# Second attention on one core: scores of a key tile added onto those of two tiles back

## The chip, the cores and the metric

One core of a Trainium2 chip runs the whole kernel in one launch. The metric is the device time of that launch in microseconds. The median of three runs is 1237.6 us (1237.28 to 1238.63).

## The reference

Two layers, each an attention times a gate, added to the tokens. 2048 tokens (2 sequences of 1024) of 128 features. Layer one is an attention over the 16 heads of a token and a mixture of experts; layer two, where the change is, is

```python
xn = _layernorm(x, axis=-1)
s = _L1_attn_ref(xn, gamma, w_qkv, w_out)      # RMS norm, then per head
#   q, k, v = rms_norm(xn) @ w_qkv ; q = q * 64 ** -0.5
#   sim = einsum('bhid,bhjd->bhij', q, k) ; attn = softmax(sim) ; out = attn @ v ; out @ w_out
g = _silu(_L1_ffn_ref(xn, ...))                # gated linear units, two hidden layers of 512
x = x + s * g
```

with 16 heads of 64 and 1024 keys for each of 1024 queries of a sequence.

## The kernel before

**Stages.** First norm, router and head attention (to about 220 us), experts (to about 350), second attention (first exponential at 369.8, last at 1084.7), last network. Products that need more than the fast format keeps are made of three: an operand is cut into a high part (F32R, a copy on ScalarE) and a low part (the rest, a subtract), and high x high, low x high and high x low are added in PSUM.

**A step** of the second attention, `m`, is one sequence and one pair of heads: 2 x 8 = 16 steps. It has 16 *slots*: `half` (512 queries) and key tile `j` (128 keys), `slot = 8 * half + j`; and 8 *batches* `b` of two slots. TensorE keeps two score banks, `st_ps[:, slot % 2]`, so that a slot's bank was last that of the slot two back. The engines' orders are written out by hand, batch by batch:

- TensorE (`tensor`): the first maxima product (`tensor_maxima`, L1273: scores of 128 queries against 512 keys into the single buffer `mx_ps`, for a later half or step), the scores of two slots (`tensor_scores`, L1286 to L1292, four products for each of the two heads: high key x high query, high x low, low x high, and minus the row maximum through `minus` and `q_max`), the second maxima product, one unit (`BEFORE`: projections q, k, k, the transposed maxima `tr`, q, v, output, `tr`), the output products of the two slots before (L1306), and in some batches a unit of `AFTER` (denominator, output, v). A maxima product waits on `s_mxr` for VectorE's reduce of the one before. The two matmuls of a line, one for each head, use different rows of the array; the text calls them a pair.
- ScalarE (`scalar`): two exponentials of 1024 columns (`prob`, L1413), then the copies out of the projection bank `pj_ps` (L1371 for `q_hi` and `k_hi`, L1376, L1383) and of `o_ps` (`o_sum`, L1389).
- VectorE (`vector`): reduce of the first maxima (L1463), reciprocals (L1481), `q_max` (L1445), reduce of the second maxima, low parts (`vector_low`, L1439), sums into `y` (L1456), and in batches 1 and 5 the normalizing multiply `o_n` (L1488), whose inputs `o_sum` and `rden` both lie in SBUF.
- GpSimd (`gpsimd`): adds the exponentials of a half into `acc` (L1550, 1024 columns, seven for each half): one in batches 0 and 4, two in each of the others.

Units of step `m + 1` (queries, keys, values) are made in step `m`. The projection bank is handed on by `bank_free`: after a `qk` unit TensorE waits for `vector_low`.

In `experts`, L903 (`x<-x,new`) and L1432 (`w_lo`, the low part of the second attention's weights) are VectorE operations with two SBUF inputs, beside GpSimd's L1052 and L1055.

Of the kernel before, what the change touches and what calls it, by code (L numbers as in the profile page):

```python
# [1067 lines left out]
def second_attention(nc, c, head, e, a, xr, xr_hi, xr_lo, early, pairs, late, at):  # L1068
# [11 lines left out]
    minus = early.sb("minus", [P, P], F32R)  # L1080
# [4 lines left out]
    q_hi, q_lo, k_hi, k_lo = ([place.sb(n, [P, LEN], F32R) for place in (pairs, late)]  # L1085
                              for n in ("q_hi", "q_lo", "k_hi", "k_lo"))
# [89 lines left out]
    def bank_free(pe, turn):  # L1176
# [5 lines left out]
        if u[0] == "qk":  # L1182
            pe.wait_ge(s_lo, 4 * q + QK.index(u) + 1)
# [207 lines left out]
    def scalar_begin(act):  # L1391
# [116 lines left out]
    def vector(dve, m, b):  # L1508
# [13 lines left out]
        if at_b and at_b[1][0] == "qk":  # L1522
# [285 lines left out]
def two_layers(nc, a, out):  # L1808

    with ExitStack() as ctx:  # L1810
# [43 lines left out]
        t2 = second_attention(nc, c, head, e, a, xr, xr_hi, xr_lo, early, pairs, late, at)  # L1854
# [258 lines left out]
```

## Time and profile before

| | |
|---|---|
| median of three runs | 1237.6 us |
| the profiled execution | 1235.84 us |
| its span | 1234.0 us |
| TensorE busy | 1177.2 us (95%) |
| VectorE busy | 850.5 us (69%) |
| GpSimd busy | 755.4 us (61%) |
| ScalarE busy | 576.3 us (47%) |
| mean granted clock of TensorE | 0.985 |

The engines run at once, each through its own list in order, and meet at semaphores. A share of busy time over the whole span mixes the stages; what bounds a stage is read from a stretch of it, and what a wait costs from the instruction that is released last. In the rows PE is TensorE (PEld its weight loads), DVE VectorE, ACT ScalarE, POOL GpSimd; L is a line of the kernel before.

### The profile page before, as it was taken

What the parts mean: (1) busy time and instruction counts of PE and PEld (TensorE: products, weight loads), DVE (VectorE), ACT (ScalarE), POOL (GpSimd) and SP (SyncE); (2) the same over time, 40 slices, a digit from 0 to 9 for tenths busy, and PEclk for the clock granted to TensorE, in tenths of its full rate; (3) what the DMA queues carried; (4) which work ended last, traced back from release to release, by engine and by line L of the source; (5) the groups of instructions that cost most, each with busy time, mean ns of one, the idle gap of its engine ahead of it and who ended that gap; (6) DMA issues with size and microseconds to landing.
All of it is one profiled execution on the core that took longest, in us unless ns stands there. A gap on an engine that the chain in (4) does not pass through costs nothing.

```text
span 1234.0 us, 22455 instructions
## 1 busy us (share of the span) xinstructions
PE 1177.2 (95%) x9276; PEld 771.4 (63%) x9276; DVE 850.5 (69%) x1062; ACT 576.3 (47%) x882; POOL 755.4 (61%) x487
## 2 busy tenths in 40 slices
PE   7999999998878999999999999999999999989997
PEld 6899999876654545555555555555555555447776
DVE  4665887566675587777777777778777777655543
ACT  1443344556535454544445445445454544544443
POOL 3565767753315577777777777787778787950000
PEclk9998999999989999999999999999999999989999
DMA  6000000020000020000000000000000000000000
GB/s 201 2 2 2 2 3 2 10 63 1 1 0 1 1 95 1 1 1 1 1 1 1 1 1 1 1 1 1 1 1 1 1 1 1 1 1 9 9 9 9
DMA packets 6981, 13.70 MB, mean 11 GB/s; under 512 B 1744, under 2 KB 4176, under 8 KB 6496
## 3 DMA queue, kind: packets, MB, share of 16 engines
q1 hardware_dynamic: 6096, 11.66, 2.8%
q8 instruction: 74, 1.21, 0.4%
q10 hardware_dynamic: 784, 0.61, 0.3%
q14 instruction: 27, 0.22, 0.1%
HBM read 11.22 MB, written 1.05 MB: 10 GB/s over the span
## 4 chain that ended last, share of the span: by engine, by line
PE 79%; DVE 11%; issue 3%; ACT 3%; POOL 3%; ACTq 1%; POOLq 0%; DVEq 0%
PE o_ps L1306 14%; PE mx_ps L1273 7%; PE ha_banks L494 6%; PE st_ps L1286 5%; PE st_ps L1288 5%; PE st_ps L1290 4%; PE st_ps L1292 4%; DVE mx_part L1463 3%; PE bank L1633 3%; PE bank L1635 3%; PE bank L1634 3%; PE pj_ps L1228 2%; POOL acc L1550 2%; PE pj_ps L1247 2%; PE pj_ps L1239 2%
## 5 line engine op out<-in xcount | busy, mean ns | idle before, releaser
L1550 POOL TENSOR_TENSOR acc<-acc,prob 128x1024 f32<-128x1024 f32 x192 | 467.0, 2432 | 127.2 <-ACT prob L1413 119.6
L1463 DVE TENSOR_REDUCE mx_part<-mx_ps 128x2 f32<-128x1024 f32 x251 | 307.3, 1224 | 127.0 <-PE mx_ps L1273 125.1
L1413 ACT ACTIVATE prob<-st_ps 128x1024 f32<-128x1024 f32 x256 | 248.8, 1024 | 211.5 <-PE st_ps L1292 211.5
L1306 PE MATMUL o_ps<-prob,v_cur 128*64 128x512 f32 x1024 | 247.7, 605 | 0.0
L1306 PEld LDWEIGHTS o_ps<-prob,v_cur 128*64 128x64 f32 x1024 | 66.6, 137 | 107.6 <-issue 104.5
L1481 DVE RECIPROCAL rden<-rden 128x128 f32<-128x128 f32 x128 | 120.2, 941 | 6.8 <-ACT rden L1383 6.8
L1273 PE MATMUL mx_ps<-k_hi,q_hi 64*128 64x512 f32 x502 | 112.3, 443 | 9.2 <-DVE mx_part L1463 8.8
L1273 PEld LDWEIGHTS mx_ps<-k_hi,q_hi 64*128 64x128 f32 x502 | 47.3, 184 | 104.4 <-issue 63.3
L1550 POOL TENSOR_TENSOR acc<-prob 128x1024 f32<-128x1024 f32 x32 | 75.9, 2371 | 54.7 <-ACT prob L1413 29.2
L1286 PE MATMUL st_ps<-q_hi,k_hi 64*128 64x512 f32 x512 | 101.7, 394 | 0.0
L1288 PE MATMUL st_ps<-q_lo,k_hi 64*128 64x512 f32 x512 | 101.1, 391 | 0.0
L1290 PE MATMUL st_ps<-q_hi,k_lo 64*128 64x512 f32 x512 | 101.0, 391 | 0.0
L1292 PE MATMUL st_ps<-q_max,minus 64*128 64x512 f32 x512 | 100.7, 389 | 0.0
L752 POOL TENSOR_TENSOR ha_wide<-ha_pt,ha_own 128x512 f32<-128x512 f32 x64 | 73.8, 1184 | 8.7 <-ACT ha_pt L709 8.7
L494 PE MATMUL ha_banks<-xn,head_wkv 128*64 128x128 f32 x1024 | 66.0, 274 | 1.5 <-DVE ha_q L599 1.0
L494 PEld LDWEIGHTS ha_banks<-xn,head_wkv 128*64 128x64 f32 x1024 | 55.0, 136 | 4.6 <-DVE ha_q L599 1.4
L1290 PEld LDWEIGHTS st_ps<-q_hi,k_lo 64*128 64x128 f32 x512 | 48.4, 185 | 11.1
L1292 PEld LDWEIGHTS st_ps<-q_max,minus 64*128 64x128 f32 x512 | 48.4, 185 | 11.0
L1288 PEld LDWEIGHTS st_ps<-q_lo,k_hi 64*128 64x128 f32 x512 | 48.3, 185 | 10.7
L1286 PEld LDWEIGHTS st_ps<-q_hi,k_hi 64*128 64x128 f32 x512 | 48.4, 186 | 9.9 <-issue 3.2
L610 DVE TENSOR_TENSOR ha_sm<-ha_banks,ha_same 128x1024 f32<-128x1024 f32 x32 | 37.6, 1216 | 24.4 <-PE ha_banks L511 24.3
L1383 ACT ACTIVATE rden<-pj_ps 128x512 f32<-128x512 f32 x32 | 19.2, 600 | 69.7 <-PE pj_ps L1239 69.7
(351 smaller groups left out, 2088.2 us busy)
## 6 DMA issues: line engine op xcount, KB each, us to landing
h_w<-in_h SPq DMA_DIRECT2D x2, 1024.0 KB, 8.4
w_raw<-in_w SPq DMA_DIRECT2D x8, 192.0 KB, 3.4
x<-in_x SPq DMA_DIRECT2D x4, 256.0 KB, 7.8
head_wkv<-in_wkv SPq DMA_DIRECT2D x1, 1024.0 KB, 12.1
out<-fin SPq DMA_DIRECT2D x4, 256.0 KB, 2.2
m_w<-in_m SPq DMA_DIRECT2D x3, 256.0 KB, 3.0
sel_raw<-in_sel SPq DMA_DIRECT2D x1, 576.0 KB, 12.1
ha_head_pos<-in_pos ACTq DMA_DIRECT2D x2, 256.0 KB, 8.8
```

The costliest lines, as they stand in the source:

```text
L494: mm = pe.matmul(pj_ps[n % 2][rows(seq), j, :], lhs, xn[:, seq * HALVES + b // TT, at_token:at_token + BLK], start=True, stop=True, skip_g ...
L752: d = pool.tensor_tensor(wide[r][:, seq, :, :, :], t.unsqueeze(3).to_broadcast([P, G // 2, HEADS, GROUPS]), own[:, :].unsqueeze(1).unsquee ...
L1273: mm = pe.matmul(to[:, h, :], q_hi[q % 2][rows(h), tile(i)], k_hi[q % 2][rows(h), half_of(keys)], start=True, stop=True)
L1286: pe.matmul(st[:, h, :], kh[rows(h), tile(j)], qh[rows(h), half_of(half)], start=True, stop=False)
L1288: pe.matmul(st[:, h, :], kh[rows(h), tile(j)], ql[rows(h), half_of(half)], start=False, stop=False)
L1290: pe.matmul(st[:, h, :], kl[rows(h), tile(j)], qh[rows(h), half_of(half)], start=False, stop=False)
L1292: mm = pe.matmul(st[:, h, :], minus[rows(h), :], q_max[rows(h), half_of(half)], start=False, stop=True)
L1306: mm = pe.matmul(o_ps[rows(h), :], v_cur[:, m % 2, j, rows(h)], prob[:, (16 * m + slot) % RING, h, :], start=(j == 0), stop=(j == KT - 1), ...
L1413: act.activation(prob[:, n % RING, :, :], st_ps[:, slot % 2, :, :], ACT.Exp, scale=SCALE).then_inc(s_exp, 1)
L1463: dve.reduce_max(mx_part[:, :, i, keys:keys + 1], maxima_banks(q, n), AX_X).then_inc(s_mxr, 1)
L1481: dve.reciprocal(part, part).then_inc(s_rcp, 1)
L1550: pool.tensor_tensor(total, old, new, ALU.add).then_inc(s_acc, 1)
```

## The change

A slot with `j` of 2 or more no longer starts its bank anew. It adds to what the bank holds, the scores of the slot two back, the product of the queries with the difference of the two key tiles: `d_hi` x high query, `d_hi` x low query, `d_lo` x high query. The row maxima are already in the bank, so their product is made only for the two *fresh* slots of a half (`j` 0 and 1, batches 0 and 4). 12 of a step's 16 slots have three pairs of matmuls in place of four; the other four keep four.

The low parts of the keys go (two VectorE subtracts of 128x512 a step out of PSUM). For them ScalarE copies the keys in full to `k_all` (128x512 twice) and makes `d_hi` (128x768); VectorE makes `d_lo` of the first 256 columns and `d_all` (768 columns) in batch 3, and the low part `d_lo` of the 768 columns (the cut) in batch 5, all from SBUF. `d_all` and `d_lo` share their place. After a key unit the projection bank is now handed on by ScalarE's `k_all`.

```diff
-def second_attention(nc, c, head, e, a, xr, xr_hi, xr_lo, early, pairs, late, at):
+def second_attention(nc, c, head, e, a, xr, xr_hi, xr_lo, early, pairs, late, spare, at):
...
-    minus = early.sb("minus", [P, P], F32R)
+    minus = spare.sb("minus", [P, P], F32R)
...
-    q_hi, q_lo, k_hi, k_lo = ([place.sb(n, [P, LEN], F32R) for place in (pairs, late)]
-                              for n in ("q_hi", "q_lo", "k_hi", "k_lo"))
+    TWO = 2 * P
+    q_hi, q_lo, k_hi, d_hi = ([place.sb(n, [P, size], F32R) for place in (pairs, late)]
+                              for n, size in (("q_hi", LEN), ("q_lo", LEN), ("k_hi", LEN), ("d_hi", LEN - TWO)))
+    d_all, d_lo = [], []
+    for place in (pairs, late):
+        d_all.append(Region(nc, place.at).sb("d_all", [P, LEN]))
+        d_lo.append(place.sb("d_lo", [P, LEN], F32R))
+    k_all = early.sb("k_all", [P, LEN])
...
@@ bank_free (TensorE: the projection bank is free after a qk unit)
-            pe.wait_ge(s_lo, 4 * q + QK.index(u) + 1)
+            _, t, half = u
+            if t:
+                pe.wait_ge(s_kall, 2 * q + half + 1)
+            else:
+                pe.wait_ge(s_lo, 2 * q + half + 1)
...
@@ tensor_scores
+            if half == 0:
+                pe.wait_ge(s_dlo, m + 1)
...
-        qh, ql, kh, kl = (t[m % 2] for t in (q_hi, q_lo, k_hi, k_lo))
+        qh, ql, kh, dh, dl = (t[m % 2] for t in (q_hi, q_lo, k_hi, d_hi, d_lo))
+        fresh = j < 2
+        if fresh:
+            for h in range(2):
+                pe.matmul(st[:, h, :], minus[rows(h), :], q_max[rows(h), half_of(half)], start=True, stop=True)
+        upper = kh[:, tile(j)] if fresh else dh[:, tile(j - 2)]
         for h in range(2):
-            pe.matmul(st[:, h, :], kh[rows(h), tile(j)], qh[rows(h), half_of(half)], start=True, stop=False)
+            pe.matmul(st[:, h, :], upper[rows(h), :], qh[rows(h), half_of(half)], start=False, stop=False,
+                      skip_group_check=True)
...
-            pe.matmul(st[:, h, :], kl[rows(h), tile(j)], qh[rows(h), half_of(half)], start=False, stop=False)
-        for h in range(2):
-            mm = pe.matmul(st[:, h, :], minus[rows(h), :], q_max[rows(h), half_of(half)], start=False, stop=True)
+            mm = pe.matmul(st[:, h, :], dl[rows(h), tile(j)], qh[rows(h), half_of(half)], start=False, stop=True,
+                           skip_group_check=True)
...
@@ scalar_unit
+            if t:
+
+                if q and half == 0:
+                    act.wait_ge(s_d, q)
+                act.activation(k_all[:, half_of(half)], qk_bank(q, u), ACT.Copy).then_inc(s_kall, 1)
...
+    def scalar_differences(act, q):
+
+        act.wait_ge(s_d, q + 1)
+        act.activation(d_hi[q % 2][:, :], d_all[q % 2][:, TWO:], ACT.Copy).then_inc(s_dhi, 1)
...
+        if b == 4 and m + 1 < STEPS:
+            scalar_differences(act, m + 1)
...
+    def vector_differences(dve, q):
+
+        dve.wait_ge(s_kall, 2 * q + 2)
+        dve.tensor_tensor(d_lo[q % 2][:, 0:TWO], k_all[:, 0:TWO], k_hi[q % 2][:, 0:TWO].bitcast(F32), ALU.subtract)
+        dve.tensor_tensor(d_all[q % 2][:, TWO:], k_all[:, TWO:], k_all[:, 0:LEN - TWO], ALU.subtract).then_inc(s_d, 1)
+
+    def vector_cut(dve, q):
+
+        dve.wait_ge(s_dhi, q + 1)
+        dve.tensor_tensor(d_lo[q % 2][:, TWO:], d_all[q % 2][:, TWO:], d_hi[q % 2][:, :].bitcast(F32), ALU.subtract)\
+           .then_inc(s_dlo, 1)
...
@@ vector_begin
-        vector_low(dve, 0, QK[1])
...
-        vector_low(dve, 0, QK[2])
...
         e.vector_norm(dve, LAST, "sum")
+        vector_differences(dve, 0)
         vector_low(dve, 0, QK[3])
-        for n in range(4, 8):
+        vector_maxima(dve, 0, 4)
+        vector_maxima(dve, 0, 5)
+        vector_cut(dve, 0)
+        for n in range(6, 8):
             vector_maxima(dve, 0, n)
...
@@ vector (one batch)
-        if at_b and at_b[1][0] == "qk":
+        if at_b and at_b[1] in (QK[0], QK[3]):
             vector_low(dve, *at_b)
...
         vector_invert(dve, m, b, 1)
+        if b == 3 and m + 1 < STEPS:
+            vector_differences(dve, m + 1)
+        if b == 5 and m + 1 < STEPS:
+            vector_cut(dve, m + 1)
...
-        early = Region(nc, HEAD + 90 * KB)
+        early = Region(nc, HEAD + 91 * KB)
         late = Region(nc, FIRST)
+        spare = Region(nc, HEAD + 56 * KB - 4 * P)
```

VectorE, from the last reduce of batch 3 of a middle step to the first of batch 6, before (`mx_part` are the reduces of maxima):

```order
L1463 TENSOR_REDUCE mx_part<-mx_ps 128x2 [waits s_mx] x2
L1481 RECIPROCAL rden<-rden 128x128
L1463 TENSOR_REDUCE mx_part<-mx_ps 128x2 [waits s_mx]
L1439 TENSOR_TENSOR q_lo<-pj_ps,q_hi 128x512 [waits s_hi]
L1481 RECIPROCAL rden<-rden 128x128
L1463 TENSOR_REDUCE mx_part<-mx_ps 128x2 [waits s_mx] x2
L1488 TENSOR_TENSOR o_n<-o_sum,rden 128x512 [waits s_rcp,s_osum,s_pj]
L1463 TENSOR_REDUCE mx_part<-mx_ps 128x2 [waits s_mx]
```

and now (the lines are those of the changed kernel: L1482 and L1483 the differences, L1488 the cut, L1538 the normalizing multiply):

```order
L1513 TENSOR_REDUCE mx_part<-mx_ps 128x2 [waits s_mx]
L1482 TENSOR_TENSOR d_lo<-k_all,k_hi 128x256 [waits s_kall]
L1483 TENSOR_TENSOR d_all<-k_all 128x768
L1513 TENSOR_REDUCE mx_part<-mx_ps 128x2 [waits s_mx]
L1531 RECIPROCAL rden<-rden 128x128
L1513 TENSOR_REDUCE mx_part<-mx_ps 128x2 [waits s_mx]
L1476 TENSOR_TENSOR q_lo<-pj_ps,q_hi 128x512 [waits s_hi]
L1531 RECIPROCAL rden<-rden 128x128
L1513 TENSOR_REDUCE mx_part<-mx_ps 128x2 [waits s_mx] x2
L1488 TENSOR_TENSOR d_lo<-d_all,d_hi 128x768 [waits s_dhi]
L1538 TENSOR_TENSOR o_n<-o_sum,rden 128x512 [waits s_rcp,s_osum,s_pj]
L1513 TENSOR_REDUCE mx_part<-mx_ps 128x2 [waits s_mx]
```

Two operations stand between the last reduce of batch 3 and the first of batch 4, without a semaphore between them, and one more between the second reduce of batch 5 and `o_n`.

TensorE, batch 5 of a middle step, its two slots' scores into `st_ps` and the second maxima product, before:

```order
L1286 MATMUL st_ps<-q_hi,k_hi 128x512 [waits s_exp]
L1286 MATMUL st_ps<-q_hi,k_hi 128x512
L1288 MATMUL st_ps<-q_lo,k_hi 128x512 x2
L1290 MATMUL st_ps<-q_hi,k_lo 128x512 x2
L1292 MATMUL st_ps<-q_max,minus 128x512 x2
L1286 MATMUL st_ps<-q_hi,k_hi 128x512 [waits s_exp]
L1286 MATMUL st_ps<-q_hi,k_hi 128x512
L1288 MATMUL st_ps<-q_lo,k_hi 128x512 x2
L1290 MATMUL st_ps<-q_hi,k_lo 128x512 x2
L1292 MATMUL st_ps<-q_max,minus 128x512 x2
L1273 MATMUL mx_ps<-k_hi,q_hi 128x512 [waits s_mxr]
```

and now:

```order
L1310 MATMUL st_ps<-q_hi,d_hi 128x512 [waits s_exp]
L1310 MATMUL st_ps<-q_hi,d_hi 128x512
L1313 MATMUL st_ps<-q_lo,d_hi 128x512 x2
L1316 MATMUL st_ps<-q_hi,d_lo 128x512 x2
L1310 MATMUL st_ps<-q_hi,d_hi 128x512 [waits s_exp]
L1310 MATMUL st_ps<-q_hi,d_hi 128x512
L1313 MATMUL st_ps<-q_lo,d_hi 128x512 x2
L1316 MATMUL st_ps<-q_hi,d_lo 128x512 x2
L1290 MATMUL mx_ps<-k_hi,q_hi 128x512 [waits s_mxr]
```

The maxima product behind the scores comes two pairs earlier in the list; its wait on `s_mxr` is the same.

## Rows read from the trace of the kernel before

**Rows 1.** The chain of waits of the whole run, shares of the span by engine.
```profile
PE 79%; DVE 11%; issue 3%; ACT 3%; POOL 3%; ACTq 1%; POOLq 0%; DVEq 0%
```

**Rows 2.** Windows: length; busy PE, PEld, DVE, ACT, POOL; granted clock; DMA.
```profile
682.00:727.00 45.00, 44.58 (x296) 23.91 (x296) 34.37 (x36) 21.86 (x27) 34.25 (x15) 1.00 0.01 1
```

**Rows 3.** TensorE in order of time: start, duration, line, operation, count, idle before.
```profile
670.46 0.50 PE L1273 MATMUL mx_ps<-k_hi,q_hi 64*128 64x512 f32 x2 [0.21 <-DVE mx_part L1463]
...
710.26 0.50 PE L1273 MATMUL mx_ps<-k_hi,q_hi 64*128 64x512 f32 x2
710.60 0.39 PE L1286 MATMUL st_ps<-q_hi,k_hi 64*128 64x512 f32 x2
710.83 0.39 PE L1288 MATMUL st_ps<-q_lo,k_hi 64*128 64x512 f32 x2
...
715.12 0.50 PE L1273 MATMUL mx_ps<-k_hi,q_hi 64*128 64x512 f32 x2 [0.21 <-DVE mx_part L1463]
715.46 0.39 PE L1286 MATMUL st_ps<-q_hi,k_hi 64*128 64x512 f32 x2
...
717.62 0.50 PE L1222 MATMUL pj_ps<-xr_hi,w_hi 128*128 128x512 f32 x1
...
718.52 1.94 PE L1306 MATMUL o_ps<-prob,v_cur 128*64 128x512 f32 x8
720.38 0.50 PE L1273 MATMUL mx_ps<-k_hi,q_hi 64*128 64x512 f32 x2
```

**Rows 4.** VectorE in order of time, batches 3 to 6.
```profile
713.85 1.22 DVE L1463 TENSOR_REDUCE mx_part<-mx_ps 128x2 f32<-128x1024 f32 x1
715.67 1.23 DVE L1463 TENSOR_REDUCE mx_part<-mx_ps 128x2 f32<-128x1024 f32 x1 [0.60 <-PE mx_ps L1273]
716.81 0.94 DVE L1481 RECIPROCAL rden<-rden 128x128 f32<-128x128 f32 x1
...
719.25 0.69 DVE L1439 TENSOR_TENSOR q_lo<-pj_ps,q_hi 128x512 fp32r<-128x512 f32 x1 [0.30 <-ACT q_hi L1371]
...
724.13 1.80 DVE L1488 TENSOR_TENSOR o_n<-o_sum,rden 128x512 f32<-128x512 f32 x1
727.01 1.23 DVE L1463 TENSOR_REDUCE mx_part<-mx_ps 128x2 f32<-128x1024 f32 x1 [1.08 <-PE mx_ps L1273]
```

**Rows 5.** GpSimd in order of time: one add alone, and pairs of adds.
```profile
700.67 2.38 POOL L1550 TENSOR_TENSOR acc<-acc,prob 128x1024 f32<-128x1024 f32 x1 [1.97 <-ACT prob L1413]
...
712.90 4.83 POOL L1550 TENSOR_TENSOR acc<-acc,prob 128x1024 f32<-128x1024 f32 x2 [1.30 <-ACT prob L1413]
...
723.02 5.15 POOL L1550 TENSOR_TENSOR acc<-acc,prob 128x1024 f32<-128x1024 f32 x2 [1.97 <-ACT prob L1413]
```

**Rows 6.** ScalarE in order of time, batch 5.
```profile
720.56 0.60 ACT L1389 ACTIVATE o_sum<-o_ps 128x512 f32<-128x512 f32 x1 [1.34 <-PE o_ps L1306]
721.85 1.94 ACT L1413 ACTIVATE prob<-st_ps 128x1024 f32<-128x1024 f32 x2 [0.69 <-PE st_ps L1292]
```

**Rows 7.** VectorE, then GpSimd, in order of time, between experts.
```profile
267.57 1.65 DVE L903 TENSOR_TENSOR x<-x,new 128x512 f32<-128x512 f32 x1
269.15 1.48 DVE L1432 TENSOR_TENSOR w_lo<-w_raw,w_hi 128x256 fp32r<-128x256 f32 x1
...
266.94 1.74 POOL L1055 TENSOR_TENSOR xm_lo<-xn,xm_hi 128x514 fp32r<-128x514 f32 x1
268.64 1.71 POOL L1052 TENSOR_TENSOR h2lo<-h,h2hi 128x512 fp32r<-128x512 f32 x1
```

**Rows 8.** TensorE in order of time; then the windows view, columns as in rows 2.
```profile
391.65 0.54 PE L1233 MATMUL pj_ps<-ident,mx_row 128*64 128x128 f32 x4 [2.46 <-ACT n1norm L881]
391.96 3.54 PE L1306 MATMUL o_ps<-prob,v_cur 128*64 128x512 f32 x8
...
392.00:395.20 3.20, 3.20 (x10) 0.70 (x6) 1.82 (x2) 0.90 (x1) 2.01 (x1) 0.50 0.00 0
```

More of the change, by code:

```diff
@@ L1105, in second_attention @@
         at.sem(n) for n in ("s_hi", "s_lo", "s_v", "s_den", "s_osum", "s_rcp", "s_on", "s_out"))
+    s_kall, s_d, s_dhi, s_dlo = (at.sem(n) for n in ("s_kall", "s_d", "s_dhi", "s_dlo"))
     BATCHES = 8
@@ L1265, in tensor_maxima @@
             elif n == 2:
-                pe.wait_ge(s_lo, 2)
+                pe.wait_ge(s_lo, 1)
+                pe.wait_ge(s_kall, 1)
         elif q == 0 and n < 8:
@@ L1283, in tensor_scores @@
         st = st_ps[:, slot % 2, :, :]
-        qh, ql, kh, kl = (t[m % 2] for t in (q_hi, q_lo, k_hi, k_lo))
+        qh, ql, kh, dh, dl = (t[m % 2] for t in (q_hi, q_lo, k_hi, d_hi, d_lo))
[4 more added lines that the diff above has]
+        upper = kh[:, tile(j)] if fresh else dh[:, tile(j - 2)]
         for h in range(2):
-            pe.matmul(st[:, h, :], kh[rows(h), tile(j)], qh[rows(h), half_of(half)], start=True, stop=False)
+            pe.matmul(st[:, h, :], upper[rows(h), :], qh[rows(h), half_of(half)], start=False, stop=False,
+                      skip_group_check=True)
         for h in range(2):
-            pe.matmul(st[:, h, :], kh[rows(h), tile(j)], ql[rows(h), half_of(half)], start=False, stop=False)
+            pe.matmul(st[:, h, :], upper[rows(h), :], ql[rows(h), half_of(half)], start=False, stop=False,
+                      skip_group_check=True)
         for h in range(2):
-            pe.matmul(st[:, h, :], kl[rows(h), tile(j)], qh[rows(h), half_of(half)], start=False, stop=False)
-        for h in range(2):
-            mm = pe.matmul(st[:, h, :], minus[rows(h), :], q_max[rows(h), half_of(half)], start=False, stop=True)
+            mm = pe.matmul(st[:, h, :], dl[rows(h), tile(j)], qh[rows(h), half_of(half)], start=False, stop=True,
+                           skip_group_check=True)
         mm.then_inc(s_st, 1)
@@ L1396, in scalar_begin @@
         scalar_unit(act, 0, QK[3])
+        scalar_differences(act, 0)
         e.scalar_norm(act, LAST, "gate")
@@ L1434, in vector_low @@
     def vector_low(dve, q, u):
-        _, t, half = u
+        part = half_of(u[2])
         dve.wait_ge(s_hi, 4 * q + QK.index(u) + 1)
-        hi, lo = (part[q % 2][:, half_of(half)] for part in ((k_hi, k_lo) if t else (q_hi, q_lo)))
-        dve.tensor_tensor(lo, qk_bank(q, u), hi.bitcast(F32), ALU.subtract).then_inc(s_lo, 1)
+        dve.tensor_tensor(q_lo[q % 2][:, part], qk_bank(q, u), q_hi[q % 2][:, part].bitcast(F32), ALU.subtract)\
+           .then_inc(s_lo, 1)
+    def vector_differences(dve, q):
[6 more added lines that the diff above has]
+           .then_inc(s_dlo, 1)
     def vector_spread_max(dve, q, u):
@@ L1850, in two_layers @@
         pairs = Region(nc, HEAD + 56 * KB)
-        early = Region(nc, HEAD + 90 * KB)
+        early = Region(nc, HEAD + 91 * KB)
         late = Region(nc, FIRST)
+        spare = Region(nc, HEAD + 56 * KB - 4 * P)
         e = experts(nc, c, first, head, x, xn, xr, xr_hi, xr_lo, eps, weights_t, moe_w, sel, at, only, keep)
-        t2 = second_attention(nc, c, head, e, a, xr, xr_hi, xr_lo, early, pairs, late, at)
+        t2 = second_attention(nc, c, head, e, a, xr, xr_hi, xr_lo, early, pairs, late, spare, at)
         behind = Region(nc, late.at)
@@ L1859, in two_layers @@
         end = last_network(nc, c, e, t2, a, x, xn, out, raw, at, token_places, Region(nc, WEIGHTS), Region(nc, HEAD + 56 * KB),
-                           Region(nc, HEAD + 90 * KB), Region(nc, FIRST))
+                           Region(nc, HEAD + 91 * KB), Region(nc, FIRST))
         BATCHES, TURNS = t2.BATCHES, head.TURNS
```

## The prediction

> **What bounds the kernel now.** I read the chain of waits first, then the engine shares of one steady step, then the time-ordered lists of two batches. The chain names TensorE for 79% of the span and VectorE for 11% [rows 1]. In the stretch 682 to 727 us, about one step of the second attention (44.66 us from 670.46, a batch 4, to 715.12, the next step's [rows 3]), TensorE is busy 44.58 of 45 us at full clock, VectorE 34.37, GpSimd 34.25, ScalarE 21.86 [rows 2]. So TensorE bounds the step; GpSimd and VectorE have some 10 us each to spare, but not at every moment. A step has 8 batches; batch 3 starts at 710.26, batch 4 at 715.12, batch 5 at 720.38 [rows 3]. Times from here on are counted from a batch's start.
>
> **What is removed on TensorE.** Inside a batch the first maxima take until 0.34 and each pair of score products adds 0.23 (710.26, 710.60, 710.83) [rows 3]. Eight pairs and the second maxima end at 2.50, where the next unit begins. Twelve of 16 slots lose one pair, so batches 1, 2, 3, 5, 6 and 7 lose 2 x 0.23 = 0.46 each; batches 0 and 4 hold the fresh slots and lose nothing. VectorE's first reduce starts 0.54 to 0.55 after the batch and lasts 1.23, ending at 1.77 [rows 3, 4]. TensorE needs 0.39 from a reduce's end to the product after the maxima (713.85 + 1.22 = 715.07, then 715.46) [rows 3, 4]. So that product comes at 2.16, not 2.04: 0.12 is given back, 0.34 stays, 2.04 a step.
>
> **What is added on ScalarE.** Per step two copies 128x512 of the keys, 0.60 each, and a copy 128x768, between that 0.60 and the 0.97 of an exponential of 1024 columns [rows 6]; by columns about 0.8. The key copies follow their twins, where the projection bank was held by a subtract on VectorE like that of 719.25, 0.69 [rows 4]: 0.60 for 0.69, nothing on the path. The 128x768 copy stands behind the o_sum copy, which runs from 0.18 to 0.78 of batch 5 [rows 3, 6]. It ends about 1.65, while the exponentials of batch 5 would begin at 1.47 - 0.23 = 1.24. They and all behind them come 0.41 late (between 0.2 and 0.6).
>
> **What is added on VectorE.** Two subtracts of 0.69 go. Three with both inputs in SBUF come: 256 and 768 columns behind the last reduce of batch 3, 768 columns behind that of batch 5, ahead of the normalizing multiply. The reduce that opens the next batch queues behind them, and TensorE's second maxima wait for it. What such an operation costs beside GpSimd decides the case.
>
> The normalizing multiply (o_n, 128x512, both inputs in SBUF) shows it: it is issued at 724.13 and ends at 725.93, the end of GpSimd's first add (723.02 plus the 2.38 of an undisturbed one, 725.40) plus 0.53; GpSimd's pair takes 5.15 where the one at 712.90 takes 4.83 [rows 4, 5]. So one waits for the whole instruction of the other. Who goes next when both wait? At 267.57 VectorE's add x<-x,new is held until xm_lo ends at 268.68 and runs to 269.22. Behind it w_lo is issued at 269.15 while GpSimd's h2lo waits since 268.64. h2lo ends at 270.35, w_lo at 270.63: GpSimd went first, and 256 columns took 0.28 [rows 7]. The engines alternate. For 768 columns I take 0.80 (0.53 + 0.28, rounded; at least 0.53, at most 1.1).
>
> The Trainium skill's page SBUF — State Buffer, section Who interferes with whom, says that VectorE's instructions with two SBUF inputs contend with a GpSimd one that reads SBUF, whoever issues first blocking the other fully. The multiply's row agrees; the page does not say who follows when both wait, and by it alone the sum could be that of the forecast or that of the rival in which VectorE keeps the port.
>
> *Batch 3 into 4.* GpSimd's pair starts at 2.64 (712.90) [rows 5], now at 2.41, since the exponential of the first slot comes one pair earlier. VectorE's second reduce was issued at 3.59 (713.85), and the operation behind a reduce starts 1.14 after it (715.67, 716.81) [rows 4]; now 3.25 and 4.39. The first add ends at 4.79, the 256 columns at 5.07, the second add at 7.45, the 768 columns at 8.25. Wherever VectorE enters, both adds and both subtracts are served by 2.41 + 4.76 + 1.08. Batch 4 starts at 4.86 - 0.34 = 4.52 and its reduce was wanted at 5.06: 3.19 late. Batch 4 is a full one with slack: reduce end 1.77 + 0.39 = 2.16 against 2.50. TensorE stalls **2.85**.
>
> *Batch 5 into 6.* The adds start at 2.64 - 0.23 + 0.41 = 2.82. First add to 5.20, the 768 columns to 6.00, second add to 8.38, the multiply's 0.53 to 8.91. Batch 6's reduce, at 727.01, was wanted 6.63 after 720.38, now 6.29, and this batch has no slack left. TensorE stalls **2.62**.
>
> Later in these batches VectorE has time to catch up (the second reduce, a reciprocal and the rest, some 3.6 us, within what TensorE still does), and GpSimd's 14 adds stay below the step. A step changes by -2.04 + 2.85 + 2.62 = +3.43. This holds for steps 1 to 14: +48.0. Step 15 prepares nothing: -2.0. Step 0 has waits for the last norm that hide both, -1 (between -2 and +3). Before step 0 VectorE gets subtracts of 0.28, 0.80 and 0.80, two of them behind ScalarE's copies, for two of 0.69: taken as +0.9. Together **+45.9**.
>
> **The clock.** The 28 new lulls are 2.6 to 2.9 us long, and the steady steps have none such. The one comparable lull in these rows, 2.46 us before 391.65, was followed by a granted clock of 0.50, the lower level of 1.2 GHz, from about 391.9 to 395.2, with the eight output products taking 3.54 instead of 1.94 [rows 3, 8]. That is some 1.6 lost if TensorE has work throughout and nothing if none falls. Part of the slow stretch may lie in the lull itself, so I take 1.2 each, nearer the row: 28 x 1.2 = **+33.6**.
>
> Sum: +79.5 on the profiled execution's 1235.84 gives 1315.3; the median 1237.6 stands 1.8 above it, so 1317.1.
>
> **Rivals.**
> 1. *Same stalls, the clock holds.* For it: two lulls of one step are surrounded by dense work. Against: rows 8. 1237.6 + 45.9 = 1283.5.
> 2. *The port is kept between the two differences, which have no semaphore wait between them, but not between cut and multiply.* The w_lo row has a wait of its own ahead of it, already met, so it may not speak for this pair. Batch 4: 4.79 + 1.08 = 5.87, 0.81 late less 0.34 slack, 0.47. A step is -2.04 + 0.47 + 2.62 = +1.05, in all 14.7 - 2.1 = +12.6 (the -2.1 being step 15, step 0 and the start), and one clock fall a step, 14 x 1.2 = +16.8: 1267.0.
> 3. *VectorE keeps the port through any run of its own operations: faster.* Batch 4 stalls 0.47; batch 6: 5.20 + 1.33 = 6.53, 0.24 late. A step is -1.33, in all -18.6 - 2.1 = -20.7: 1216.9. It is decided by who is served after VectorE's first subtract; the sign turns once the two stalls together pass 2.04. Against it stand rows 7.
> 4. *The change does not come through*: the products dropped are hidden and nothing is contended. TensorE's 44.58 of 45 us speaks against it; within 0.2% of 1237.6.
>
> **Chances.** A measurement of this kernel can tell about 0.2% (2.5 us) from no change. Forecast 0.60, rival 1 0.12, rival 2 0.10, rival 3 0.13, rival 4 0.03, and 0.02 for something slower than all. Faster 0.14 (rival 3 and a trace of others), same 0.03, slower 0.83. The range runs from 1250, rival 2 without a clock fall, to 1336: all 28 lulls at 1.6 give 1328, and 8 us are for the copies' and step 0's upper bounds. Rivals 3 and 4 are left out.
>
> **What would show it.** Right: a steady step of about 50.5 us; the reduce opening batch 4 and that opening batch 6 each 2.6 to 3.2 us later than now against the batch's start; d_all at about 3.2 us and the normalizing multiply behind the cut at about 2.9 us for work of 0.8 and 0.5; TensorE idle before maxima, released by VectorE, some 75 us in all; the granted clock at 0.50 in parts of each step. Wrong in the port term: both differences done in 1.5 us. Wrong in the clock term: 1.00 throughout with those stalls there. If second maxima in batches 1, 2, 3 and 7 are held by much more than 0.12, the gain term is wrong.

## Result and the profile after

The changed kernel takes 1315.41 us (median of four runs, 1302.86 to 1327.97) against 1237.44 us of the kernel before measured beside it. The ratio of the runs is 1.0552, 95% interval [1.0505, 1.0599]; it rests on the two lower runs, as every ratio here leaves out executions more than 1.5% above the fastest of their kernel, such as a few of 1642 to 4390 us in the first session below, whose medians still count them. A repeat on another occasion, below, gave 1325.2 us and 1.0709 [1.0689, 1.0729]. The forecast was 1317.1 us. The profiled execution took 1323.27 us, its span 1321.5 us, mean granted clock 0.953.

In the rows of the changed kernel L1290 is the maxima product, L1331 the outputs, L1263 the output projection, L1482 and L1483 the low difference of 256 columns and d_all, L1488 the cut, L1513 the reduce, L1538 the normalizing multiply, L1606 GpSimd's adds of the softmax sum. The chain of waits, where [rows 1] stood:

```profile
PE 65%; DVE 24%; issue 5%; ACT 3%; POOL 2%; ACTq 1%; POOLq 0%; DVEq 0%
```

VectorE's share grew from 11% to 24%. Engine shares of one step, and of two pieces of it (length, busy time of each engine with its instructions, then the granted clock), against [rows 2]:

```profile
core 0: us, PE busy (x) PEld busy (x) DVE busy (x) ACT busy (x) POOL busy (x), PEclk, DMA share, GB/s
702.30:753.50 51.20, 46.48 (x268) 21.98 (x268) 39.90 (x38) 23.09 (x29) 34.36 (x15) 0.93 0.00 1
708.00:711.70 3.70, 3.70 (x12) 0.78 (x10) 2.28 (x3) 0.60 (x1) 0.23 (x1) 0.54 0.00 0
722.00:726.00 4.00, 4.00 (x12) 1.16 (x14) 3.03 (x5) 0.00 (x0) 2.79 (x2) 0.60 0.00 0
```

The step went from 44.66 to 51.20 us. TensorE, with 24 matmuls less, is busy 46.48 us, and in two pieces most of the time is at the lower level of its clock. TensorE in time order, batches 4, 5 and 6 (starting at 702.32, 711.69 and 717.53), against [rows 3]:

```profile
702.32 0.50 PE L1290 MATMUL mx_ps<-k_hi,q_hi 64*128 64x512 f32 x2 [0.21 <-DVE mx_part L1513]
706.84 0.51 PE L1290 MATMUL mx_ps<-k_hi,q_hi 64*128 64x512 f32 x2 [2.19 <-DVE mx_part L1513]
708.17 3.59 PE L1331 MATMUL o_ps<-prob,v_cur 128*64 128x512 f32 x8
711.69 0.50 PE L1290 MATMUL mx_ps<-k_hi,q_hi 64*128 64x512 f32 x2
713.51 0.49 PE L1290 MATMUL mx_ps<-k_hi,q_hi 64*128 64x512 f32 x2
717.53 0.50 PE L1290 MATMUL mx_ps<-k_hi,q_hi 64*128 64x512 f32 x2
721.43 0.52 PE L1290 MATMUL mx_ps<-k_hi,q_hi 64*128 64x512 f32 x2 [2.01 <-DVE mx_part L1513]
721.87 1.97 PE L1263 MATMUL pj_ps<-o_n,wo 128*64 128x512 f32 x4
723.63 2.66 PE L1331 MATMUL o_ps<-prob,v_cur 128*64 128x512 f32 x8
```

The second maxima of batches 4 and 6 start 4.52 and 3.90 us after their batch, released by VectorE; those of batch 5 at 1.82. The idle time just before the two late ones, 2.19 and 2.01 us, is called a lull. Behind both lulls the clock is low: eight output products take 3.59 and 2.66 us, where at full clock they take 1.94 or 1.89. VectorE in those batches, against [rows 4]:

```profile
702.17 0.41 DVE L1482 TENSOR_TENSOR d_lo<-k_all,k_hi 128x256 fp32r<-128x256 f32 x1
702.51 3.14 DVE L1483 TENSOR_TENSOR d_all<-k_all 128x768 f32<-128x768 f32 x1
705.58 1.21 DVE L1513 TENSOR_REDUCE mx_part<-mx_ps 128x2 f32<-128x1024 f32 x1
...
715.19 2.25 DVE L1488 TENSOR_TENSOR d_lo<-d_all,d_hi 128x768 fp32r<-128x768 f32 x1
717.36 2.87 DVE L1538 TENSOR_TENSOR o_n<-o_sum,rden 128x512 f32<-128x512 f32 x1
720.16 1.22 DVE L1513 TENSOR_REDUCE mx_part<-mx_ps 128x2 f32<-128x1024 f32 x1
```

GpSimd's pairs of adds, against [rows 5], and ScalarE at the start of batch 5, against [rows 6]:

```profile
699.94 4.90 POOL L1606 TENSOR_TENSOR acc<-acc,prob 128x1024 f32<-128x1024 f32 x2 [1.05 <-ACT prob L1449]
...
714.25 5.43 POOL L1606 TENSOR_TENSOR acc<-acc,prob 128x1024 f32<-128x1024 f32 x2 [6.02 <-ACT prob L1449]
```

```profile
711.87 0.60 ACT L1424 ACTIVATE o_sum<-o_ps 128x512 f32<-128x512 f32 x1 [3.00 <-PE o_ps L1331]
712.36 0.84 ACT L1418 ACTIVATE d_hi<-d_all 128x768 fp32r<-128x768 f32 x1
713.09 1.93 ACT L1449 ACTIVATE prob<-st_ps 128x1024 f32<-128x1024 f32 x2
```

The first pair of adds spans 4.90 us; an add alone takes 2.37 to 2.38. The 256 columns end at 702.58, 0.27 behind the first add's end at 702.31; d_all starts its turn only behind the second and ends at 705.65, 0.81 after the pair's end at 704.84. The reduce of batch 4 is issued 3.26 us after its batch starts instead of 0.54, that of batch 6 2.63. That is the forecast's mechanism, in place and in nearly its size. The experiments below test it.

### The profile page after: what moved, and what is told of

It reads as the page before. It is cut to its first block, busy times and chain, and to the rows that moved or that the text cites. A ratio compares the mean times of both kernels' runs of the same rounds, so it can differ in the third digit from the quotient of the medians.

```text
span 1321.5 us, 21752 instructions
## 1 busy us (share of the span) xinstructions
PE 1194.2 (90%) x8892; PEld 741.7 (56%) x8892; DVE 936.5 (71%) x1078; ACT 601.0 (45%) x930; POOL 763.2 (58%) x487
## 4 chain that ended last, share of the span: by engine, by line
PE 65%; DVE 24%; issue 5%; ACT 3%; POOL 2%; ACTq 1%; POOLq 0%; DVEq 0%
PE o_ps L1331 13%; PE mx_ps L1290 7%; DVE mx_part L1513 6%; PE ha_banks L494 6%; DVE d_all L1483 3%; DVE o_n L1538 3%; PE bank L1689 3%; PE st_ps L1316 3%; PE pj_ps L1263 3%; PE st_ps L1313 3%; PE st_ps L1310 3%; DVE d_lo L1488 3%; PE bank L1691 2%; PE bank L1690 2%; POOL acc L1606 2%
## 5 line engine op out<-in xcount | busy, mean ns | idle before, releaser
L1606 POOL TENSOR_TENSOR acc<-acc,prob 128x1024 f32<-128x1024 f32 x192 | 474.8, 2473 | 176.3 <-ACT prob L1449 168.2
L1513 DVE TENSOR_REDUCE mx_part<-mx_ps 128x2 f32<-128x1024 f32 x251 | 303.2, 1208 | 135.1 <-PE mx_ps L1290 134.7
L1331 PE MATMUL o_ps<-prob,v_cur 128*64 128x512 f32 x1024 | 273.6, 659 | 0.0
L1290 PE MATMUL mx_ps<-k_hi,q_hi 64*128 64x512 f32 x502 | 125.7, 497 | 71.0 <-DVE mx_part L1513 70.5
L1290 PEld LDWEIGHTS mx_ps<-k_hi,q_hi 64*128 64x128 f32 x502 | 47.7, 186 | 211.2 <-DVE mx_part L1513 137.0
L1331 PEld LDWEIGHTS o_ps<-prob,v_cur 128*64 128x64 f32 x1024 | 72.2, 149 | 127.5 <-issue 119.7
L1606 POOL TENSOR_TENSOR acc<-prob 128x1024 f32<-128x1024 f32 x32 | 75.8, 2369 | 56.5 <-ACT prob L1449 44.4
L1316 PE MATMUL st_ps<-q_hi,d_lo 64*128 64x512 f32 x512 | 101.6, 391 | 0.0
L1310 PE MATMUL st_ps<-q_hi,d_hi 64*128 64x512 f32 x384 | 75.9, 391 | 0.0
L1313 PE MATMUL st_ps<-q_lo,d_hi 64*128 64x512 f32 x384 | 75.8, 390 | 0.0
L1538 DVE TENSOR_TENSOR o_n<-o_sum,rden 128x512 f32<-128x512 f32 x32 | 70.1, 2191 | 0.4
L1406 ACT ACTIVATE v_cur<-pj_ps 128x512 f32<-128x512 f32 x32 | 19.2, 599 | 93.0 <-PE pj_ps L1244 92.2
L1316 PEld LDWEIGHTS st_ps<-q_hi,d_lo 64*128 64x128 f32 x512 | 48.7, 185 | 10.8
L683 ACT ACTIVATE ha_v<-ha_banks,ha_head_bv 128x128 f32<-128x128 f32 x128 | 35.5, 375 | 32.4 <-PE ha_banks L494 32.4
L1029 DVE TENSOR_TENSOR su<-sg,u_ps 128x512 f32<-128x512 f32 x32 | 21.9, 686 | 38.1 <-ACT sg L1002 19.9
L1424 ACT ACTIVATE o_sum<-o_ps 128x512 f32<-128x512 f32 x32 | 19.1, 598 | 62.0 <-PE o_ps L1331 62.0
```

Of the source, the lines that this page charges most:

```text
L1290: mm = pe.matmul(to[:, h, :], q_hi[q % 2][rows(h), tile(i)], k_hi[q % 2][rows(h), half_of(keys)], start=True, stop=True)
L1310: pe.matmul(st[:, h, :], upper[rows(h), :], qh[rows(h), half_of(half)], start=False, stop=False, skip_group_check=True)
L1313: pe.matmul(st[:, h, :], upper[rows(h), :], ql[rows(h), half_of(half)], start=False, stop=False, skip_group_check=True)
L1316: mm = pe.matmul(st[:, h, :], dl[rows(h), tile(j)], qh[rows(h), half_of(half)], start=False, stop=True, skip_group_check=True)
L1331: mm = pe.matmul(o_ps[rows(h), :], v_cur[:, m % 2, j, rows(h)], prob[:, (16 * m + slot) % RING, h, :], start=(j == 0), stop=(j == KT - 1), ...
L1513: dve.reduce_max(mx_part[:, :, i, keys:keys + 1], maxima_banks(q, n), AX_X).then_inc(s_mxr, 1)
```

## Experiments

In the expectations A is the explanation of the forecast: the shared port and the turns on it make the opening reduces of batches 4 and 6 late, TensorE stalls, and the clock falls behind each lull. B says that VectorE's own added work costs the time, C that the clock costs nothing of its own; D is told where it stands. Every kernel was timed beside the kernel before, whose median in the three sessions was 1235.63, 1236.19 and 1237.01 us.

**The dropped products alone.** The differences are made for steps 0 and 1 only.

```diff
...
-        if b == 4 and m + 1 < STEPS:
+        if b == 4 and m + 1 < 2:
             scalar_differences(act, m + 1)
...
-        if b == 3 and m + 1 < STEPS:
+        if b == 3 and m + 1 < 2:
             vector_differences(dve, m + 1)
...
-        if b == 5 and m + 1 < STEPS:
+        if b == 5 and m + 1 < 2:
             vector_cut(dve, m + 1)
```

> The kernel after the change, but the differences of keys (three subtracts on VectorE, the 128x768 copy on ScalarE) are made for steps 0 and 1 only; the later steps use those stale ones, so what is computed from step 2 on is not the reference's. The key copies into k_all stay. It shows what the dropped products bring when nothing is added on VectorE. Theory A (the added subtracts, through the port they share with GpSimd, cost all of the loss): the batches 1, 2, 5, 6, 7 keep the 0.24 to 0.34 seen in the trace of the change, about 1.3 us a step, no lull before batches 4 and 6 and no fall of the clock: 1216 to 1220 us. Rival B (something else of the change costs, such as the k_all copies or the new start of a slot): well above 1237.

Measured: 1219.94 us, ratio 0.9871 [0.9846, 0.9897]. The step is 43.37 us, 1.30 below the 44.66 of before. TensorE in batches 1 and 3 of a step:

```profile
646.28 0.50 PE L1290 MATMUL mx_ps<-k_hi,q_hi 64*128 64x512 f32 x2
...
648.11 0.50 PE L1290 MATMUL mx_ps<-k_hi,q_hi 64*128 64x512 f32 x2
648.54 0.50 PE L1238 MATMUL pj_ps<-xr_hi,w_hi 128*128 128x512 f32 x1
...
658.03 0.50 PE L1290 MATMUL mx_ps<-k_hi,q_hi 64*128 64x512 f32 x2
...
659.85 0.51 PE L1290 MATMUL mx_ps<-k_hi,q_hi 64*128 64x512 f32 x2
660.45 0.44 PE L1249 MATMUL pj_ps<-ident,mx_row 128*64 128x128 f32 x4
```

In batch 1, and alike in batches 2, 5, 6 and 7, the next unit begins 2.26 us after the batch (648.54), not 2.50: 0.24 kept out of 0.46. In batch 3 the transpose begins at 2.42, only 0.08 earlier: the bank it needs is free when VectorE's add into y has ended, 0.06 before it. Five times 0.24 and 0.08 are 1.28 of the 1.30. So the rest of the change (the k_all copies, the new opening of a slot) is not what costs the time; it lies in the differences, on VectorE or beside it. (The copy `d_hi` on ScalarE is gone here too; in the runs below it is there.)

**GpSimd's adds left out,** in the changed kernel and in the kernel before.

```diff
-        pool.tensor_tensor(total, old, new, ALU.add).then_inc(s_acc, 1)
+        if m == 0 and j == 1:
+            pool.memset(total, 1.0).then_inc(s_acc, 1)
+        else:
+            pool.memset(total[:, :, 0:1], 1.0).then_inc(s_acc, 1)
```

> The change with GpSimd's adds of the softmax sum left out (a memset of one column stands in each one's place, so the denominators are not the reference's). Theory A (the port): without the adds the three subtracts take 0.3 and 0.8 us, the reduces that open batches 4 and 6 are late by 0.5 to 0.8 at most, 1217 to 1224 us. Rival B (VectorE's own work): the time stays near 1290 to 1315.

> The kernel before the change with the same adds left out, as the base for the one above. Both theories: the adds hide beside TensorE there, so 1235 to 1238 us.

Measured: 1216.38 us, ratio 0.985 [0.9825, 0.9876], and for the base 1234.01, 0.9991 [0.9976, 1.0006]. Both lie just below what was expected. All of VectorE's added work is there, and the change is now faster by 17.6 us than its base; its step is 43.63 us, 0.27 above the 43.37 of the kernel without differences, which is what that work costs without the adds. Taking the adds away is worth nothing before the change and 99 us after it (109 by the repeat). The differences by line (count, then shortest, median and longest in ns, then the first and last start in us) in the changed kernel without adds:

```profile
L1483 DVE TENSOR_TENSOR d_all<-k_all x16: 952/952/952, 360.9 to 1016.9; 128x768 f32<-128x768 f32 x16
```

and in the changed kernel itself:

```profile
L1483 DVE TENSOR_TENSOR d_all<-k_all x16: 945/3151/3155, 356.5 to 1109.2; 128x768 f32<-128x768 f32 x16
L1488 DVE TENSOR_TENSOR d_lo<-d_all,d_hi x16: 945/2243/3007, 360.3 to 1121.8; 128x768 fp32r<-128x768 f32 x16
```

Work of 0.95 us takes 3.15 beside the adds. B has fallen: the cost is that the two engines meet. The Trainium skill's page SBUF — State Buffer, section Who interferes with whom, calls the shared port an exclusive lock held for the whole instruction by whoever issues first; by the 0.95 and 3.15 above the trace agrees.

**Idle products in the lulls,** so that TensorE waits working.

```diff
+        if b in (4, 6) and 1 <= m < STEPS - 1:
+            turn = turn_of[before(m, b)]
+            bank_free(pe, turn)
+            for i in range(8):
+                pe.matmul(pj_ps[:, :], k_hi[m % 2][:, tile(0)], q_hi[m % 2][:, half_of(0)], start=True, stop=True, skip_group_check=True)
```

> The change with eight idle products more (keys by queries of the running step into a free projection bank, about 1.9 us, read by nobody) placed ahead of the second maxima of batches 4 and 6 in steps 1 to 14, where TensorE stood waiting for VectorE. The stalls stay what they are, only TensorE isn't idle in them. Theory A (a lull costs by itself and again by the lower clock level behind it): granted clock 1.00 throughout these steps, the step about 48.7 instead of 51.2 us, 1280 to 1290 us. Rival C (the slow stretch costs nothing of its own, as it lies beside other waits): unchanged, 1310 to 1320 us.

Measured: 1288.11 us (1284.49 to 1290.11), ratio 1.042 [1.0392, 1.0448]. TensorE does 2.1 us more work twice a step, and the kernel is 27 us faster than the changed one (37 than its repeat). Two steps of it, one before and one after the eighth:

```profile
650.00:698.00 48.00, 47.33 (x288) 24.36 (x288) 39.91 (x38) 23.12 (x29) 34.42 (x14) 1.00 0.00 1
841.00:889.70 48.70, 47.34 (x287) 24.22 (x284) 40.59 (x38) 23.54 (x31) 35.83 (x15) 1.00 0.00 1
```

The clock stays at 1.00, and the stalls are the old ones: the unit behind the second maxima comes 4.97 and 4.31 us after batches 4 and 6, against 4.96 and 4.34 in the changed kernel. C has fallen. This kernel also shows the stalls without the clock: the step is 47.92 us, +3.26 on before, and 51.2 with the falls, so a fall costs (51.2 - 47.92) / 2 = 1.64 us. The profiled execution understates the gain: its second attention starts 4.4 us later than the changed kernel's (first `o_sum` at 407.36 against 402.96), in stages that are the same code in both; from there to the last `o_sum` of a batch 5 it takes 718.2 us against 755.9, 37.7 less.

**The cut moved away** from the normalizing multiply, to batch 7.

```diff
+        if b == 7 and m + 1 < STEPS:
+            vector_cut(dve, m + 1)
...
-        if b == 5 and m + 1 < STEPS:
-            vector_cut(dve, m + 1)
```

> The change with the cut alone moved, from the end of batch 5 (ahead of the normalizing multiply) to behind the first reduce of batch 7. Theory A: the stall before the maxima of batch 6 (2.30 us) and its fall of the clock (about 1.25 us) go, 14 times each, so about 46 to 50 us less, 1265 to 1272 us; batch 4 unchanged. Rival B (total work of VectorE): unchanged at about 1315.

Measured: 1274.36 us, ratio 1.0303 [1.0271, 1.0335]. The step is 47.5 us, 3.7 less: the stall of batch 6 and one fall. From the 1315.41 it is 41 us, from the repeat's 1325.2 it is 51, so A's 46 to 50 lies between; the time itself is 2 us above the range of 1265 to 1272.

**One subtract instead of two** between the reduces that close batch 3 and open batch 4; the 256 columns follow the latter.

```diff
...
     def vector_differences(dve, q):
...
-        dve.tensor_tensor(d_lo[q % 2][:, 0:TWO], k_all[:, 0:TWO], k_hi[q % 2][:, 0:TWO].bitcast(F32), ALU.subtract)
...
+    def vector_first_low(dve, q):
+        dve.tensor_tensor(d_lo[q % 2][:, 0:TWO], k_all[:, 0:TWO], k_hi[q % 2][:, 0:TWO].bitcast(F32), ALU.subtract)\
+           .then_inc(s_d, 1)
...
+        if b == 4 and m + 1 < STEPS:
+            vector_first_low(dve, m + 1)
...
```

> The change with the difference of 256 columns moved from ahead of d_all (end of batch 3) to behind the first reduce of batch 4, so that only one subtract stands between the last reduce of batch 3 and the first of batch 4. Theory A (the engines take turns, so two subtracts span a whole add and one does not): d_all waits for the end of the first add only and ends at about 5.6 after the start of batch 3 instead of 8.2, the stall of batch 4 falls from 2.46 to 0.3 or less, one fall of the clock a step goes, about 1265 us (1258 to 1275). If instead the turn goes by which engine asked first in each case and GpSimd's second add already stands in line, the stall stays and the time with it, about 1315. Rival B (total work): unchanged.

Measured: 1266.14 us, ratio 1.0239 [1.0206, 1.0272]. VectorE and then GpSimd around that place:

```profile
679.68 1.22 DVE L1516 TENSOR_REDUCE mx_part<-mx_ps 128x2 f32<-128x1024 f32 x1
680.81 0.95 DVE L1482 TENSOR_TENSOR d_all<-k_all 128x768 f32<-128x768 f32 x1
681.67 1.22 DVE L1516 TENSOR_REDUCE mx_part<-mx_ps 128x2 f32<-128x1024 f32 x1
682.81 1.50 DVE L1485 TENSOR_TENSOR d_lo<-k_all,k_hi 128x256 fp32r<-128x256 f32 x1
```

```profile
678.57 5.45 POOL L1612 TENSOR_TENSOR acc<-acc,prob 128x1024 f32<-128x1024 f32 x2 [1.05 <-ACT prob L1449]
```

d_all meets the end of the first add (678.57 + 2.37 = 680.94), goes ahead of the second and takes 0.95 instead of 3.14; the 256 columns, alone behind a reduce, now wait for the second add's end at 684.02 and end at 684.31. Batch 4 has no stall. One subtract ahead of a reduce is served between two adds; in the changed kernel it is the second of the two that pays a whole add. TensorE in batches 5 and 6, and two steps by window:

```profile
643.35 0.50 PE L1290 MATMUL mx_ps<-k_hi,q_hi 64*128 64x512 f32 x2 [0.56 <-DVE mx_part L1516]
650.47 0.50 PE L1290 MATMUL mx_ps<-k_hi,q_hi 64*128 64x512 f32 x2 [1.21 <-DVE mx_part L1516]
```

```profile
640.90:686.40 45.50, 43.09 (x270) 21.53 (x270) 37.67 (x38) 23.15 (x30) 34.79 (x15) 1.00 0.01 1
825.00:873.00 48.00, 44.84 (x270) 21.95 (x268) 38.58 (x39) 23.63 (x30) 36.18 (x16) 0.96 0.00 1
```

In steps 2 to 7 more went than A said: batch 5 has a stall of 0.55 now, the lull of batch 6 is 1.21 instead of 2.01, no fall of the clock follows it, and the step is 45.46 us, 5.7 less. From step 8 on the lull of batch 6 is 1.98 to 2.29 again, with a fall behind it, and the step is 47.8 to 48.2. So the 1265 us were met with the right stall of batch 4, but partly by luck in the rest. Taking turns, as the forecast read [rows 7], and serving whoever asked first give the same order in every row here and were not told apart.

**The maxima product put back into all slots.**

```diff
-        if fresh:
-            for h in range(2):
-                pe.matmul(st[:, h, :], minus[rows(h), :], q_max[rows(h), half_of(half)], start=True, stop=True)
+        for h in range(2):
+            pe.matmul(st[:, h, :], minus[rows(h), :], q_max[rows(h), half_of(half)], start=fresh, stop=True,
+                      skip_group_check=True)
```

> The change with the product that subtracts the maxima put back into all 16 slots (so the scores are not the reference's): 12 pairs of 0.23 us a step more on TensorE, 16 steps, 44 us of TensorE work in all. Theory A (in batches 1, 2, 3, 5, 6 and 7 the time saved is partly handed back to waits, 0.24 of 0.46 stayed in each): 4 to 6 batches pay 0.24 each and batch 6 hides its own in the stall, 1.0 to 1.5 us a step, 1330 to 1340 us. If all of the saving counted, +2.8 a step, about 1359 us. If none did, 1315 us.

Measured: 1320.15 us, ratio 1.068 [1.0651, 1.0709]: +4.7 us on the changed kernel, -5 on its repeat. This was a miss; none of the three sums gives it, the 1315 that comes nearest for another reason. Up to step 8 the steps are 50.4 to 50.7 us and twice 48.9, against 51.2, and from there on 51.2 to 52.9, against 47.9 to 52.2. Lulls of one step:

```profile
651.96 0.50 PE L1290 MATMUL mx_ps<-k_hi,q_hi 64*128 64x512 f32 x2 [2.33 <-DVE mx_part L1513]
666.60 0.49 PE L1290 MATMUL mx_ps<-k_hi,q_hi 64*128 64x512 f32 x2 [1.32 <-DVE mx_part L1513]
```

and of its steps by window:

```profile
606.37:656.94 50.57, 46.49 (x294) 24.02 (x296) 40.13 (x37) 23.23 (x29) 34.22 (x14) 0.97 0.00 1
656.94:705.90 48.96, 44.89 (x294) 23.67 (x296) 39.86 (x37) 23.26 (x30) 34.18 (x14) 1.00 0.00 1
```

With more work in the batches its lull is 1.32 instead of 2.01 us, and in these steps one fall at most is left (0.97 and 1.00 instead of 0.93); a step with one and a step with none are 1.6 us apart. At full clock the step is 48.9, 1.0 above the 47.92 of the kernel with idle products, which is what A gave; the fall that went pays for it. The expectation had left the clock out.

**Both moved,** to where GpSimd has no add running: the differences behind the first reduce of batch 5, d_hi in batch 6, the cut behind the first reduce of batch 7.

```diff
-        if b == 4 and m + 1 < STEPS:
+        if b == 6 and m + 1 < STEPS:
             scalar_differences(act, m + 1)
...
+        if b == 5 and m + 1 < STEPS:
+            vector_differences(dve, m + 1)
+        if b == 7 and m + 1 < STEPS:
+            vector_cut(dve, m + 1)
...
-        if b == 3 and m + 1 < STEPS:
-            vector_differences(dve, m + 1)
-        if b == 5 and m + 1 < STEPS:
-            vector_cut(dve, m + 1)
```

> The same work as the change, other places: the first low difference and d_all move from the end of batch 3 to behind the first reduce of batch 5, the copy d_hi to batch 6, the cut behind the first reduce of batch 7, where GpSimd has no add running by the trace of the change. Theory A (port and alternation make them long only beside the adds): each subtract of 768 columns takes about 0.8 us instead of 2.3 to 3.2, no stall of TensorE before the maxima of batches 4 and 6, full clock, 1216 to 1222 us, faster than both. Rival B (VectorE's own added work of 1.9 us a step is what is too much, wherever it stands): above 1290.

Measured: 1232.82 us, ratio 0.9971 [0.9956, 0.9987]: faster than both, but by 3 us, not by 15 or more. Seven steps take the 43.36 us of the kernel without differences, the next six 45.6 to 45.9. VectorE and GpSimd in batch 5 of the first slow one:

```profile
799.69 1.26 DVE L1482 TENSOR_TENSOR d_lo<-k_all,k_hi 128x256 fp32r<-128x256 f32 x1
800.87 3.12 DVE L1483 TENSOR_TENSOR d_all<-k_all 128x768 f32<-128x768 f32 x1
```

```profile
799.37 1.29 POOL L1759 TENSOR_TENSOR m_lo<-m_w,m_hi 128x512 fp32r<-128x512 f32 x1 [0.70 <-ACT m_hi L1754]
800.62 5.58 POOL L1606 TENSOR_TENSOR acc<-acc,prob 128x1024 f32<-128x1024 f32 x2
```

From step 8 on GpSimd splits a tile of the last stage's weights once a step, behind the add of batch 4. It holds the port when the 256 columns want it, and the turns do the rest.

**That split moved as well,** with its copy on ScalarE, from batch 4 to batch 0.

```diff
-            return m - PAIRS if b == 4 and 0 <= m - PAIRS < end.EARLY else None
+            return m - PAIRS if b == 0 and 0 <= m - PAIRS < end.EARLY else None
```

> The kernel with both places moved, and one thing more: the split of the last stage's weights (a copy on ScalarE and a 128x512 subtract on GpSimd, one per step from step 8 on) moves from batch 4 to batch 0. In the trace without this, steps up to the eighth take 43.36 us and from then on 45.6 to 45.9, and the first such GpSimd subtract runs from 799.37 to 800.66 just where VectorE wants its differences, which then take 1.26 and 3.12 us instead of 0.42 and 0.95. Theory A (the port and its turns, whoever holds it): every steady step 43.4 us, 7 to 8 steps times 2.3 less, 1216 to 1220 us, as fast as the kernel with the products dropped and no differences made. Rival D (something else of the later steps, such as the DMA of the last stage's weights or ScalarE's copy, takes the 2.3 us): 1229 to 1235 us, unchanged.

Measured: 1218.53 us (1215.53 to 1220.69), ratio 0.985 [0.9827, 0.9873]. Every steady step is 43.40 us, and six times 2.3 us is the 14 us by which the kernel is shorter than the one before it. The same place:

```profile
800.43 0.42 DVE L1482 TENSOR_TENSOR d_lo<-k_all,k_hi 128x256 fp32r<-128x256 f32 x1
800.76 0.95 DVE L1483 TENSOR_TENSOR d_all<-k_all 128x768 f32<-128x768 f32 x1
```

Of D the DMA has fallen: its transfers were not moved. ScalarE's copy moved along with the subtract, so the run by itself does not part the two; the row of 799.69 does, which ends at 800.95, 0.29 behind the end of GpSimd's subtract at 800.66, as with an operation held by it. This version computes everything the reference asks for and beats both kernels, 18.5 us below the one before and 97 below the change as made (107 by the repeat).

**The changed kernel once more.**

> The changed kernel unaltered, once more, since its four runs lay between 1303 and 1328 us, wider than any other. Theory A (the clock falls behind a lull in some steps and not in others, 27 lulls at 1.3 to 1.7 us each): again a spread of 15 to 25 us, 1303 to 1330 us, and in the profile steps of about 51.2 us with two falls, 49.6 to 50 with one and 47.9 to 48.7 with none. If the spread was chance of another kind, all runs within 0.5% of one value.

Measured: 1325.2 us (1323.92 to 1325.95), ratio 1.0709 [1.0689, 1.0729]. The spread of 15 to 25 us that was expected did not come: the four lie within 0.2% of each other; its steps are the profiled ones of before (51.20 with two falls up to step 8, then 47.94 to 52.3). What made two of the first four runs some 20 us shorter wasn't settled: their mean granted clock was 0.963 and 0.967 against 0.951 to 0.954 in the long ones, which speaks for fewer falls, but no profile of a short one was taken.

## Why the prediction was right, point by point

The forecast of 1317.1 us stands 1.7 from the median and 8 from the repeat. Its mechanism was the right one: the port, the turns, the two stalls and the falls of the clock are all in the rows. That it came so near is luck in part: the median lies between two runs near 1305 and two near 1325, and the terms err both ways and cancel.

- **What bounds the kernel**: right. Without stalls each step follows TensorE's work.
- **The gain term, 2.04 a step**: mis-sized, 1.30 measured. The step "so that product comes at 2.16" failed. It took its 0.39 from the first maxima of a batch, with a score pair behind them; behind held second maxima the unit comes 0.48 after the reduce's end (648.54 after 648.06). Batch 3 was taken like the others, but there the add into y is next and leaves 0.08. The sign named for this term, second maxima held by much more than 0.12, did not show it: they start at 1.83, held by some 0.11, and another 0.11 is lost between them and the unit (0.43 where it was 0.32).
- **ScalarE**: right. d_hi takes 0.84 (0.8); the exponentials of batch 5 start 1.40 after the batch (1.65, where 1.24 was undisturbed).
- **One waits for the whole instruction of the other, the engines take turns**: right, except that turns and first come, first served were not told apart. d_all 3.14 (3.2), the normalizing multiply behind the cut 2.87 (2.9).
- **Stall of batch 4, 2.85 forecast**: the unit behind the maxima comes 4.96 after the batch instead of 2.50, 2.46. **Stall of batch 6, 2.62**: 4.34 instead of an unstalled 2.26, 2.08, or 2.30 over the 2.04 from which the forecast counted. The reduces are late by 2.72 and 2.09; the second lies outside the 2.6 to 3.2 given. Half of what it lacks is that the adds of batch 5 start at 2.56 and not at 2.82; the rest is in three small terms (a batch 5 of 5.84 us and not 5.75, the adds and operations 5.98 and not 6.09 together, and a reduce that is issued 0.07 before the multiply ends).
- **The step, +3.43 without the clock**: +3.26 in the kernel with idle products; a gain too large and stalls too large nearly cancel (-1.30 + 2.46 + 2.08 = +3.24).
- **All steps alike**: wrong from step 8 on, where the split of the last stage's weights (a copy on ScalarE, a subtract on GpSimd) lengthens the step by another 0.77 at full clock (48.69 for 47.92), in most of six steps, 3.8 us together. The whole without the clock is 1288.1 - 1236.2 = 51.9 where 45.9 was forecast; but of the 54.2 us between the two profiled spans only 46.9 lie between the first and the last `o_sum` of a batch 5, and the start later by 4.4 us than in the changed kernel's own profile is not the change's. So this term came out nearer than the medians say.
- **The clock, 1.2 a lull, 33.6 in all**: a fall costs 1.64, the 1.6 of [rows 8] in full, of which the forecast had struck a quarter; in later steps some lulls bring none. In all 27 us against the first median, 37 against the repeat and 37.7 within the second attention of the two profiles, where 33.6 was forecast.
- **Idle before maxima released by VectorE**: 70.5 us where some 75 were said.
- **Rival 1** (clock holds, 1283.5) is in effect the kernel with idle products, 1288.1. **Rivals 2 and 3** fell with d_all's 3.14 and with the multiply's 2.87. Rival 3's time, 1216.9, is what better places reach (1218.5). **Rival 4** fell.

## What to carry to other kernels

Here an operation of VectorE with two SBUF inputs cost its own length only where GpSimd had no add running or one just about to end (0.95 us for 768 columns); the second of two in a row beside two adds paid a whole add (3.14). Before adding such work, list GpSimd's instructions at that place in every phase of the loop, rare ones too: here the same operations in other batches turned +5.5% to +7.1% into -0.3%, and with one GpSimd subtract and its ScalarE copy moved too, into -1.5%. Where a stall of TensorE can't be avoided, count the lower clock behind it as part of its price: here 1.64 us behind most lulls of 2 us.

## What the runs showed that was not expected

- Adding TensorE work made the kernel faster: 28 groups of eight products that nobody reads took 27 to 37 us off, by keeping the clock at 1.00.
- Twelve pairs of real products more a step changed the time by about 5 us either way, in part since a lull of 1.32 us in place of 2.01 was not followed by a fall. Lulls of 2.0 and 2.2 mostly were; those of 1.2 in two other kernels were not. Each is a count of rows here and no law.
- Leaving out 224 GpSimd adds, 543 us of its work in the kernel before and 551 in the changed one, was worth nothing in the former (0.9991 [0.9976, 1.0006]) and about 99 us in the latter.
